# A graph network's third stage: projection from two half-state tiles, and a new order of work on four engines

## The chip, the cores and the metric

The kernel runs on one core of a Trainium2 chip. The metric is device time of one execution, in microseconds. Four engines compute: TensorE (PE) multiplies matrices, VectorE (DVE) and ScalarE (ACT) work elementwise, GpSimd (POOL) issues the gathers and scatters. SyncE (SP) issues the other transfers, which 16 DMA engines carry out. Each engine takes its own instructions in order and waits on semaphores for the others.

## The reference

Four graph layers follow each other over 100,000 nodes with 64 features and 50,000 edges. Before each layer the node state is normed: h = relu(layernorm(x)). The change lies in the third stage of the kernel, which ends the second layer and prepares the third:

```python
# second layer, its end: out is the sum over a node's edges
out = (out - mean) * rsqrt(var + eps) * gamma + beta
x = x + gelu(out + h)                       # exact gelu
# third layer, its start
h = relu(layernorm(x))
qkv = h @ qkv_w + qkv_b
qe = q[src] * 8 ** -0.5 + edge_attr @ q_rpe_w + q_rpe_b
ke = k[dst] + edge_attr @ k_rpe_w + k_rpe_b
ve = v[dst] + edge_attr @ v_rpe_w + v_rpe_b
compat = sum over 8 of qe * ke              # 4 heads
```

## The kernel before

The program runs stage by stage; between stages all engines meet. The stage in question is `conv_edges` (scope `l2`, L1588 to L1783). The edges are sorted by destination and cut into 98 **chunks** of CE = 512. A chunk's state is held turned: 64 features of the source node in partitions 0 to 63, 64 of the destination in 64 to 127, 512 edges as columns.

For a chunk, in this order: SyncE loads the edges' own rows, `keep`, and the turned states `h1` and `x1`; GpSimd gathers the rows of the destination's last edge. TensorE transposes the rows into `p_oT` (L1782). VectorE runs a scan backwards over the destination half (L1708), so that all edges of a node get its sum, and forms z = p_oT * scale + h1 (L1720). ScalarE applies gelu (L1679). VectorE adds x1: x2 (L1704). TensorE centers x2 with one matmul over 512 columns (L726), ScalarE squares (L730), TensorE averages the squares (L734, the variance), ScalarE makes 1/sqrt of it with Ln and Exp (L741, L743), VectorE scales and clips to `hT` (L748). TensorE also transposes x2 back (L1771), VectorE copies it to rows (L1728) and SyncE stores it. The 18 edge attributes with a column of ones are transposed to 32 x 512 (L1021) and copied to `ea.T` by VectorE (L1732). The **projection** takes, for each of four tiles of 128 edges, two matmuls into the same 128 columns: hT (128 rows) with `w_qkv` (L1747), and 19 rows of ea.T with `w_rpe`, added to it (L1748). ScalarE copies the result out: queries and keys `qk` (L1672), values `vc` (L1673). VectorE multiplies queries and keys (L1714) and sums over 8 (L1723); SyncE stores `vc`.

Gelu is in another table set of ScalarE than Ln and Exp, so a set is loaded (L205) before the gelu and one after it.

The order is written out by hand. The helper `slots` lets every engine run through slots; in slot s a body gets the chunks s, s-1, s-2 and so on (k0, k1, k2 ...), None where there is none. Before the change SyncE loads chunk s; TensorE works on s-2 (center, variance, back), s-4 (projection in two halves, the variance between them) and s (transposes); ScalarE on s-3 (Ln, Exp), s-5 (copies out), s-2 (square), s-1 (gelu); VectorE on s-2 (x2), s-1 (scan, z), s-5 (product, sum), s-3 (row copy, attributes, scaling). Two slots are a turn. `p_oT`, `p_back`, `p_ea`, `n_p_var` and, before, `z` are single buffers; most others are double (`u`), the loaded ones fourfold (`q`). `hold` is a wait with an empty instruction behind it.

## Time and profile before

| | us |
|---|---|
| median of the runs | 6815.0 |
| lowest and highest of 3 | 6811.4, 6820.2 |
| the profiled execution, its own time | 6795.7 |
| its span in the profile | 6793.8 |
| the stage's scans, first to last | 2861.4 to 3544.5 |

The profile is of one execution. Its time is 19 us under the median; 2 us of it lie outside the span. Busy shares over the whole span are TensorE 62%, VectorE 69%, ScalarE 49%, GpSimd 66%, but they are averages over stages with different limits, so the stage has to be read by itself.

### The profile page before, as it was taken

To read this page: it belongs to the slowest core of one execution; us is meant where nothing else is said; L and a number is where in the kernel's file an instruction comes from. 1 tells how busy PE (TensorE), PEld (TensorE's weight loads), DVE (VectorE), ACT (ScalarE), POOL (GpSimd) and SP (SyncE) were. 2 spreads that over 40 slices of the span, in tenths; PEclk is the share of its full clock that TensorE was granted. 3 is DMA by queue.
4 is the path that set the end of the run, shared out by engine and by line. 5 is a ranking of instruction groups with operands and counts; after the bars stand their busy time and mean duration, and the time that the engine had idled before them with its cause. 6 is when DMAs were issued, how large, how long until landed. Compare 5 with 4: busy or idle time off the path is not lost. (4 is left out here: it accounts for less than half of the span.)

```text
span 6793.8 us, 85831 instructions
## 1 busy us (share of the span) xinstructions
PE 4193.3 (62%) x15111; PEld 2135.7 (31%) x15111; DVE 4701.1 (69%) x9073; ACT 3325.8 (49%) x5670; POOL 4502.1 (66%) x4877
## 2 busy tenths in 40 slices
PE   0102555555477777699996777775777677777700
PEld 0000211111133333266663333332434344444400
DVE  5885888888577777576664555555777667766667
ACT  1112444444355555487885666665777733333300
POOL 4777888888644444265546888886766477777744
PEclk9999999999999999799997888887999978778855
DMA  2442222222344444499983344443333233333377
GB/s 89 140 144 56 81 74 74 78 74 74 83 132 131 132 132 129 104 186 193 192 178 93 114 114 114 114 114 93 75 80 78 65 66 71 69 71 69 69 297 309
DMA packets 949964, 773.07 MB, mean 114 GB/s; under 512 B 661199, under 2 KB 727708, under 8 KB 945875
## 3 DMA queue, kind: packets, MB, share of 16 engines
q1 hardware_dynamic: 819859, 614.72, 30.6%
q0 software_dynamic: 125504, 131.83, 12.2%
q10 hardware_dynamic: 4512, 25.60, 0.9%
q14 instruction: 66, 0.54, 0.0%
q8 instruction: 23, 0.38, 0.0%
HBM read 472.43 MB, written 310.28 MB: 115 GB/s over the span
## 5 line engine op out<-in xcount | busy, mean ns | idle before, releaser
L205 ACT ACT_TABLE_LOAD x621 | 796.7, 1283 | 139.3 <-PEq L66 128.6
L954 POOL DMA_INDIRECT x<-l_out,l_snum x392 | 472.5, 1205 | 106.5 <-issue 90.1
L918 POOL DMA_INDIRECT l_rows<-x,l_num x392 | 441.2, 1126 | 153.5 <-issue 93.7
L954 POOL DMA_INDIRECT m<-l2s_out,l2s_snum x392 | 439.2, 1120 | 146.5 <-issue 105.7
L1159 POOL DMA_INDIRECT pre_src_rows<-in_x,all_idx_src x392 | 397.2, 1013 | 164.3 <-issue 130.0
L918 POOL DMA_INDIRECT l_rows<-in_x,l_num x392 | 432.1, 1102 | 105.7 <-issue 90.6
L918 POOL DMA_INDIRECT l3a_rows<-m,l3a_num x392 | 398.6, 1017 | 144.3 <-issue 93.3
L918 POOL DMA_INDIRECT l2s_rows<-vc_rows,l2s_num x392 | 416.5, 1062 | 106.3 <-issue 95.5
L918 POOL DMA_INDIRECT l_rows<-eo,l_num x392 | 387.5, 989 | 147.7 <-issue 96.7
L954 POOL DMA_INDIRECT xg<-l3b_out,l3b_snum x392 | 395.2, 1008 | 113.2 <-issue 90.3
L918 POOL DMA_INDIRECT l3b_rows<-g_rows,l3b_num x392 | 385.6, 984 | 106.2 <-issue 92.4
L837 DVE TENSOR_TENSOR_SCAN l2s_sums<-l2s_ex,l2s_sums 128x512 f32<-128x512 f32 x97 | 124.6, 1284 | 458.3 <-ACT l2s_ex L828 458.3
L1349 PE MATMUL l_p_hT<-all_ident,l_h 128*128 128x128 f32 x392 | 109.2, 433 | 468.5 <-DVE l_h L681 468.5
L2407 PE MATMUL l3b_p_gate<-all_w_gate,l3b_acc 128*128 128x256 f32 x784 | 305.4, 557 | 32.5 <-DVEq L2366 31.4
L310 ACT ACTIVATE prep_pay<-prep_pay 128x512 f32<-128x512 f32 x136 | 85.7, 630 | 416.9 <-DVEq L396 416.9
L734 PE MATMUL l_n_p_var<-l_n_sq,all_w_mean 128*128 128x512 f32 x392 | 220.7, 645 | 95.9 <-ACT l_n_sq L730 95.6
L2399 PE MATMUL l3b_p<-all_ident,l3b_hm 128*128 128x128 f32 x392 | 126.6, 345 | 231.0 <-DVEq L2359 231.0
L1349 PEld LDWEIGHTS l_p_hT<-all_ident,l_h 128*128 128x128 f32 x392 | 70.0, 217 | 631.6 <-DVE l_h L681 631.6
L432 PE MATMUL prep_ptk<-all_ident,prep_key 128*128 128x128 f32 x72 | 20.1, 434 | 402.2 <-DVEq L382 402.2
L1981 PE MATMUL l2s_p_score<-l2s_vT,all_w_head 68*128 68x512 f32 x196 | 110.3, 645 | 238.9 <-ACT l2s_vT L1918 238.9
L1708 DVE TENSOR_TENSOR_SCAN l_p_oT<-l_keep,l_end_T,l_p_oT 64x512 f32<-64x512 f32 x98 | 127.5, 1301 | 185.5 <-PE l_p_oT L1782 148.2
L2454 POOL TENSOR_TENSOR dl_min<-dl_min,all_shift 128x1600 f32<-128x1600 f32 x32 | 131.2, 4099 | 182.7 <-DMA dl_min<-m 182.7
(407 smaller groups left out, 13700.1 us busy)
## 6 DMA issues: line engine op xcount, KB each, us to landing
l_far<-far_d SPq DMA_DIRECT2D x196, 256.0 KB, 3.4
xg<-l2s_bg_row SPq DMA_DIRECT2D x97, 512.0 KB, 3.8
dl_xin<-xg SPq DMA_DIRECT2D x31, 1600.0 KB
l2s_bg_x<-x SPq DMA_DIRECT2D x97, 260.0 KB, 3.0
x<-ts_row SPq DMA_DIRECT2D x31, 812.5 KB, 4.4
l_keep<-keep_d SPq DMA_DIRECT2D x196, 128.0 KB, 2.9
xs<-l_xT SPq DMA_DIRECT2D x98, 256.0 KB, 2.7
hs<-l_hT SPq DMA_DIRECT2D x98, 256.0 KB, 3.0
```

The costliest lines, as they stand in the source:

```text
L205: act.add_instruction(mybir.InstLoadActFuncSet(name=nc.get_next_instruction_name(), ins=[], outs=[], act_func_set_id=which))
L734: pe.matmul(self.p_var[:], c.w_mean[:], self.sq[:], start=True, stop=True).then_inc(self.spread, 1)
L837: dve.tensor_tensor_scan(self.sums[k.u][:], self.ex[:, 0, :], self.ex[:, 1, :], 0.0 if k.start else self.sums[1 - k.u][:, CE - 1:CE], ALU. ...
L918: pool.indirect_dma_start(self.buf[k.q][:, j, at:at + w], None, table, bass.IndirectOffsetOnAxis(ap=self.num[k.q][:, m, j:j + 1], axis=0)) ...
L954: pool.indirect_dma_start(self.table, bass.IndirectOffsetOnAxis(ap=self.num[k.q][:, j:j + 1], axis=0), self.out[k.q][:, j, 0:self.cols], N ...
L1159: pool.indirect_dma_start(c.src_rows[:, t, :], None, x, bass.IndirectOffsetOnAxis(ap=c.idx_src[:, t:t + 1], axis=0)).then_inc(c.src_gather ...
L1349: ins = pe.transpose(p_hT[:, j * P:(j + 1) * P], h[:, j, :], c.ident[:])
L1708: swept = step(dve.tensor_tensor_scan(p_oT[D:P, ::-1], keep[k1.q][D:P, ::-1], p_oT[D:P, ::-1], end_T[D:P, bass.ds(k1.i, 1)], ALU.mult, ALU ...
L1981: pe.matmul(p_score[k1.u][:], c.w_head[:], vT[k1.u][:], start=True, stop=True).then_inc(m["scored"], 1)
L2399: pe.transpose(p_01[:, cols], hm[:, j, 0:P], c.ident[:])
L2407: ins = pe.matmul(p_gates[:, j, :], acc[k1.u][:, j * P:(j + 1) * P], c.w_gate[:], start=True, stop=True)
L2454: pool.tensor_tensor(min_[k.u][:], min_[k.u][:], over_rows(c.shift3[0:NP, :], NR), ALU.add).then_inc(pool_done, 1)
```

## The change

Destination and source half of the normed state go to two tiles, each of which also holds the attributes: `from_src` has the source half in partitions 0 to 63 and the attributes in 64 to 95; `from_dst` has the attributes in 0 to 31 and the destination half in 64 to 127, with zeros between. The weights are copied together once to match (`w_q`, `w_kv`). The projection is then, for each tile, one matmul of 96 rows into 32 columns (the queries) and one of 128 rows into 96 columns (keys and values), neither added to the other. VectorE scales in two instructions (`scale_halves`); ScalarE copies the attributes, twice, in place of VectorE's one copy. z gets a second buffer. Gelu of chunk s-2 stands at the end of ScalarE's even slots and at the start of the odd ones, so that two gelus share one table load. Center, variance, square and what follows move by one slot; the variance becomes TensorE's last work in a slot, the new chunk's transposes stand ahead of it, and the projection is in one piece. ScalarE's copies out stand behind the square. SyncE loads x1 and the attributes two slots after the rows.

```diff
+    def scale_halves(self, dve, k, top, bottom):
+
+        dve.wait_ge(self.scaled, k.n)
+        cen, rstd = self.of(self.p_cen, k), self.of(self.rstd, k)
+        dve.scalar_tensor_tensor(top[0:D, :], cen[0:D, :], 0.0, rstd[0:D, :], ALU.max, ALU.mult)
+        dve.scalar_tensor_tensor(bottom[D:P, :], cen[D:P, :], 0.0, rstd[D:P, :], ALU.max, ALU.mult).then_inc(self.done, 1)
...
-        z, hT = s.sb("z", [P, CE]), [s.sb(f"hT{u}", [P, CE]) for u in range(2)]
+        z = [s.sb(f"z{u}", [P, CE]) for u in range(2)]
+        from_src, from_dst = ([s.sb(f"{n}{u}", [P, CE]) for u in range(2)] for n in ("from_src", "from_dst"))
+        w_q, w_kv = s.sb("w_q", [P, 32]), s.sb("w_kv", [P, 96])
...
-        ea = EdgeAttr(s, edge_attr, ATTR, 1, both=True)
+        ea = EdgeAttr(s, edge_attr, ATTR, 1)
...
-                def body(k, k1, _2, _3, old, _5, _6, older):
+                def body(k, _1, k2, _3, _4, old, _6, _7, older):
...
-                        if not k.round:
-                            hold(sp, m["x2_ready"], k.n - 4)
-                        sp.dma_start(x1[k.q][:], feature_rows(xs, k)).then_inc(x1_loaded[k.q], 16)
+                    if k2:
+                        if not k2.round:
+                            hold(sp, m["x2_ready"], k2.n - 4)
+                        sp.dma_start(x1[k2.q][:], feature_rows(xs, k2)).then_inc(x1_loaded[k2.q], 16)
                     if old:
                         hold(sp, m["rows_ready"], old.n)
                         sp.dma_start(edge_rows(x2e, old), x2_rows[old.u][:]).then_inc(x2_saved[old.u], 16)
...
-                    if k1:
-                        ea.load(sp, c, k1)
-                slots(sp, c.NCH, 7, body)
+                    if k2:
+                        ea.load(sp, c, k2)
+                slots(sp, c.NCH, 8, body)
...
-                def body(k1, k2, k3, k5):
+                def gelu(k):
+                    act.wait_ge(m["z_ready"], k.n)
+                    act.activation(z[k.u][:], z[k.u][:], ACT.Gelu, bias=c.shift1T[:, 0:1]).then_inc(m["gelu_done"], 1)
+
+                def attributes(k):
+                    if not k.first:
+                        act.wait_ge(m["qkv_done"], k.n - 2)
+                    act.wait_ge(ea.turned, k.n)
+                    act.activation(from_src[k.u][D:D + 32, :], ea.p[:], ACT.Copy)
+                    act.activation(from_dst[k.u][0:32, :], ea.p[:], ACT.Copy).then_inc(ea.ready, 1)
...
+                def out(k):
+                    if not k.first:
+                        act.wait_ge(m["vc_ready"], k.n - 2)
+                    if not k.round:
+                        act.wait_ge(vc_saved[k.q], 16 * k.r)
+                    act.wait_ge(m["qkv_done"], k.n)
+                    v = p_qkv[k.u][:].rearrange("p (j f) -> p j f", j=TPC)
+                    act.activation(qk[k.u][:], v[:, :, 0:D], ACT.Copy)
+                    act.activation(vc[k.q][:, :, 0:D], v[:, :, D:P], ACT.Copy).then_inc(m["qkv_out"], 1)
+
+                def even(k2, k3, k4, k6):
+                    if k4:
+                        norm.rsqrt(act, c, k4)
+                    load_set(nc, act, GELU_SET)
+                    if k4:
+                        attributes(k4)
                     if k3:
-                        norm.rsqrt(act, c, k3)
-                    if k5:
-                        if not k5.first:
-                            act.wait_ge(m["vc_ready"], k5.n - 2)
-                        if not k5.round:
-                            act.wait_ge(vc_saved[k5.q], 16 * k5.r)
-                        act.wait_ge(m["qkv_done"], k5.n)
-                        v = p_qkv[k5.u][:].rearrange("p (j f) -> p j f", j=TPC)
-                        act.activation(qk[k5.u][:], v[:, :, 0:D], ACT.Copy)
-                        act.activation(vc[k5.q][:, :, 0:D], v[:, :, D:P], ACT.Copy).then_inc(m["qkv_out"], 1)
-                    load_set(nc, act, GELU_SET)
-                    if k2:
-                        norm.square(act, k2)
-                    if k1:
-                        act.wait_ge(m["z_ready"], k1.n)
-                        act.activation(z[:], z[:], ACT.Gelu, bias=c.shift1T[:, 0:1]).then_inc(m["gelu_done"], 1)
+                        norm.square(act, k3)
+                    if k6:
+                        out(k6)
+                    if k2:
+                        gelu(k2)
+
+                def odd(k2, k3, k4, k6):
+                    if k2:
+                        gelu(k2)
                     load_ln_exp(nc, act)
-                slots(act, c.NCH, 5, lambda k0, k1, k2, k3, k4, k5: body(k1, k2, k3, k5))
+                    if k4:
+                        attributes(k4)
+                    if k3:
+                        norm.square(act, k3)
+                    if k4:
+                        norm.rsqrt(act, c, k4)
+                    if k6:
+                        out(k6)
+                calls = [0]
+
+                def body(_0, _1, k2, k3, k4, _5, k6):
+                    calls[0] += 1
+                    (even if calls[0] % 2 else odd)(k2, k3, k4, k6)
+                slots(act, c.NCH, 6, body)
...
+                for w_ in (w_q, w_kv):
+                    early(dve.memset(w_[:], 0.0))
+                early(dve.tensor_copy(w_q[0:D, :], c.w_qkv[0:D, 0:32]))
+                early(dve.tensor_copy(w_q[D:D + ATTR + 1, :], c.w_rpe[0:ATTR + 1, 0:32]))
+                early(dve.tensor_copy(w_kv[0:ATTR + 1, :], c.w_rpe[0:ATTR + 1, 32:P]))
+                early(dve.tensor_copy(w_kv[D:P, :], c.w_qkv[D:P, 32:P]))
+                for u in range(2):
+                    early(dve.memset(from_dst[u][:], 0.0))
...
+                def body(k1, k3, k4, k6):
+                    if k3:
+                        if not k3.first:
+                            dve.wait_ge(m["back_turned"], k3.n - 2)
+                        dve.wait_ge(x1_loaded[k3.q], 16 * (k3.r + 1))
+                        dve.wait_ge(m["gelu_done"], k3.n)
+                        dve.tensor_tensor(x2[k3.u][:], z[k3.u][:], x1[k3.q][:], ALU.add).then_inc(m["x2_ready"], 1)
                     if k1:
                         dve.wait_ge(keep_loaded[k1.q], 16 * (k1.r + 1))
                         dve.wait_ge(rows.rows_free, k1.n)
                         swept = step(dve.tensor_tensor_scan(p_oT[D:P, ::-1], keep[k1.q][D:P, ::-1], p_oT[D:P, ::-1],
                                                             end_T[D:P, bass.ds(k1.i, 1)], ALU.mult, ALU.add))
...
+                    if k6:
+                        if not k6.start:
+                            dve.wait_ge(m["vc_ready"], k6.n - 1)
+                        dve.wait_ge(m["qkv_out"], k6.n)
+                        multiplied = step(dve.tensor_tensor(prod[:].rearrange("p j h f -> p j (h f)"), qk[k6.u][:, :, 0:32],
+                                                            qk[k6.u][:, :, 32:64], ALU.mult))
                     if k1:
                         step.ended(swept)
                         dve.sem_inc(m["keep_used"], 1)
+                        if not k1.first:
+                            dve.wait_ge(m["x2_ready"], k1.n - 2)
                         dve.wait_ge(h1_loaded[k1.q], 16 * (k1.r + 1))
-                        dve.scalar_tensor_tensor(z[:], p_oT[:], c.scale1T[:, 0:1], h1[k1.q][:], ALU.mult, ALU.add).then_inc(m["z_ready"], 1)
-                    if k5:
+                        dve.scalar_tensor_tensor(z[k1.u][:], p_oT[:], c.scale1T[:, 0:1], h1[k1.q][:], ALU.mult, ALU.add).then_inc(m["z_ready"], 1)
+                    if k6:
                         step.ended(multiplied)
...
+                        dve.tensor_reduce(vc[k6.q][:, :, D:VC], prod[:], AX, ALU.add).then_inc(m["vc_ready"], 1)
+                    if k4:
+                        if not k4.first:
+                            dve.wait_ge(x2_saved[k4.u], 16 * k4.t)
+                        dve.wait_ge(m["back_turned"], k4.n)
+                        dve.tensor_copy(x2_rows[k4.u][:].rearrange("p j f -> p (j f)"), p_back[:]).then_inc(m["rows_ready"], 1)
+                        if not k4.first:
+                            dve.wait_ge(m["qkv_done"], k4.n - 2)
+                        norm.scale_halves(dve, k4, from_src[k4.u], from_dst[k4.u])
+                slots(dve, c.NCH, 6, lambda k0, k1, k2, k3, k4, k5, k6: body(k1, k3, k4, k6), step)
...
-                hold(pe, m["early_step"], 8)
+                hold(pe, m["early_step"], 16)
...
                 def project(k, tiles):
                     for j in tiles:
                         at = slice(j * P, (j + 1) * P)
-                        pe.matmul(p_qkv[k.u][:, at], hT[k.u][:, at], c.w_qkv[:], start=True, stop=False)
-                        ins = pe.matmul(p_qkv[k.u][:, at], ea.T[k.u][0:ATTR + 1, at], c.w_rpe[:], start=False, stop=True)
+                        pe.matmul(p_qkv[k.u][:, j * P:j * P + 32], from_src[k.u][0:D + 32, at], w_q[0:D + 32, :], start=True, stop=True)
+                        ins = pe.matmul(p_qkv[k.u][:, j * P + 32:(j + 1) * P], from_dst[k.u][:, at], w_kv[:], start=True, stop=True)
                     return ins
...
-                def body(k0, k1, k2, k3, k4):
-                    if k2:
-                        hold(pe, m["x2_ready"], k2.n)
-                        norm.center(pe, c, k2, x2[k2.u][:])
-                    if k4:
-                        if not k4.first:
-                            hold(pe, m["qkv_out"], k4.n - 2)
-                        hold(pe, ea.ready, k4.n)
-                        hold(pe, norm.done, k4.n)
-                        project(k4, (0, 1))
-                    if k2:
-                        if k3:
-                            hold(pe, norm.logged, k3.n)
-                        norm.variance(pe, c, k2)
-                    if k4:
-                        project(k4, (2, 3)).then_inc(m["qkv_done"], 1)
-                    if k2:
-                        if k3:
-                            hold(pe, m["rows_ready"], k3.n)
+                def body(k0, k1, _2, k3, k4, k5):
+                    if k3:
+                        hold(pe, m["x2_ready"], k3.n)
+                        norm.center(pe, c, k3, x2[k3.u][:])
+                    if k5:
+                        if not k5.first:
+                            hold(pe, m["qkv_out"], k5.n - 2)
+                        hold(pe, ea.ready, k5.n)
+                        hold(pe, norm.done, k5.n)
+                        project(k5, range(TPC)).then_inc(m["qkv_done"], 1)
+                    if k3:
+                        if k4:
+                            hold(pe, m["rows_ready"], k4.n)
                         for j in range(TPC):
-                            ins = pe.transpose(p_back[:, j * P:(j + 1) * P], x2[k2.u][:, j * P:(j + 1) * P], c.ident[:])
+                            ins = pe.transpose(p_back[:, j * P:(j + 1) * P], x2[k3.u][:, j * P:(j + 1) * P], c.ident[:])
                         ins.then_inc(m["back_turned"], 1)
-                        if k3:
-                            hold(pe, ea.ready, k3.n)
-                        ea.turn(pe, c, k2)
                     if k0:
                         if k1:
                             hold(pe, m["z_ready"], k1.n)
@@ -1781,7 +1822,14 @@
                         for j in range(TPC):
                             ins = pe.transpose(p_oT[:, j * P:(j + 1) * P], rows.buf[k0.q][:, j, :], c.ident[:])
                         ins.then_inc(rows.rows_free, 1)
-                slots(pe, c.NCH, 4, body)
+                    if k3:
+                        if k4:
+                            hold(pe, ea.ready, k4.n)
+                        ea.turn(pe, c, k3)
+                        if k4:
+                            hold(pe, norm.logged, k4.n)
+                        norm.variance(pe, c, k3)
+                slots(pe, c.NCH, 5, body)
```

On ScalarE, the steady part of the stage, before: one slot. Names end in the buffer's number; `l2_n_sq` is the square, `l2_n_rstd` Ln and Exp, `l2_z` gelu, `l2_qk` and `l2_vc` the copies out.

```order
L741 ACTIVATE l2_n_rstd0<-l2_n_p_var,all_eps 128x512
L743 ACTIVATE l2_n_rstd0<-l2_n_rstd0 128x512
L1672 ACTIVATE l2_qk0<-l2_p_qkv0 128x256
L1673 ACTIVATE l2_vc0<-l2_p_qkv0 128x4x64
L205 ACT_TABLE_LOAD
L730 ACTIVATE l2_n_sq<-l2_n_p_cen1 128x512
L1679 ACTIVATE l2_z<-l2_z,all_shift1T 128x512
L205 ACT_TABLE_LOAD
```

After, from the copies out of an even slot to those of the odd one behind it (`from_src`, `from_dst` are the attribute copies):

```order
L1690 ACTIVATE l2_qk0<-l2_p_qkv0 128x256
L1691 ACTIVATE l2_vc2<-l2_p_qkv0 128x4x64
L1674 ACTIVATE l2_z0<-l2_z0,all_shift1T 128x512
L1674 ACTIVATE l2_z1<-l2_z1,all_shift1T 128x512
L205 ACT_TABLE_LOAD
L1680 ACTIVATE l2_from_src1<-l2_p_ea 32x512
L1681 ACTIVATE l2_from_dst1<-l2_p_ea 32x512
L730 ACTIVATE l2_n_sq<-l2_n_p_cen0 128x512
L741 ACTIVATE l2_n_rstd1<-l2_n_p_var,all_eps 128x512
L743 ACTIVATE l2_n_rstd1<-l2_n_rstd1 128x512
L1690 ACTIVATE l2_qk1<-l2_p_qkv1 128x256
L1691 ACTIVATE l2_vc3<-l2_p_qkv1 128x4x64
```

The copies out stand behind the square now; in the odd slot behind Ln and Exp too, and one table load stands between two gelus and the next Ln.

On TensorE, the same part, one slot before (`l2_p_oT` are the transposes of the new chunk, `l2_p_back` those of x2):

```order
L1747 MATMUL l2_p_qkv1<-all_w_qkv,l2_hT1 128x128
L1748 MATMUL l2_p_qkv1<-all_w_rpe,l2_eaT1 128x128
L1747 MATMUL l2_p_qkv1<-all_w_qkv,l2_hT1 128x128
L1748 MATMUL l2_p_qkv1<-all_w_rpe,l2_eaT1 128x128
L734 MATMUL l2_n_p_var<-l2_n_sq,all_w_mean 128x512
L1747 MATMUL l2_p_qkv1<-all_w_qkv,l2_hT1 128x128
L1748 MATMUL l2_p_qkv1<-all_w_rpe,l2_eaT1 128x128
L1747 MATMUL l2_p_qkv1<-all_w_qkv,l2_hT1 128x128
L1748 MATMUL l2_p_qkv1<-all_w_rpe,l2_eaT1 128x128
L1771 MATMUL l2_p_back<-all_ident,l2_x2_1 128x128 x4
L1021 MATMUL l2_p_ea<-all_ident,l2_ea1 32x128 x4
L1782 MATMUL l2_p_oT<-all_ident,l2_rows1 128x128 x4
```

And after, the end of one slot, with the last tile's projection, from which the next slot follows with the center (the first row is a keys-and-values matmul of the slot):

```order
L1798 MATMUL l2_p_qkv1<-l2_w_kv,l2_from_dst1 128x96
L1797 MATMUL l2_p_qkv1<-l2_w_q,l2_from_src1 128x32
L1798 MATMUL l2_p_qkv1<-l2_w_kv,l2_from_dst1 128x96
L1815 MATMUL l2_p_back<-all_ident,l2_x2_1 128x128 x4
L199 REGISTER_ALU
L1823 MATMUL l2_p_oT<-all_ident,l2_rows2 128x128 x4
L1028 MATMUL l2_p_ea<-all_ident,l2_ea1 32x128 x4
L734 MATMUL l2_n_p_var<-l2_n_sq,all_w_mean 128x512
```

The variance has moved from the projection's middle to the slot's end, behind the back-transposes, the new chunk's transposes and the attributes.

## Rows read from the trace of the kernel before

**Rows 1.** Instructions of the tile p_oT: min/median/max ns, first and last start in us.

```profile
L1708 DVE TENSOR_TENSOR_SCAN l_p_oT<-l_keep,l_end_T,l_p_oT x98: 1300/1301/1302, 2861.4 to 3544.5; 64x512 f32<-64x512 f32 x98
```

**Rows 2.** Timeline 3205 to 3216: start us, us, engine, line, operation, count [idle before <-releaser].

```profile
3207.53 0.69 ACT L741 ACTIVATE l_n_rstd<-l_n_p_var,all_eps 128x512 f32<-128x512 f32 x1 [0.22 <-PE l_n_p_var L734]
...
3208.25 0.63 ACT L743 ACTIVATE l_n_rstd<-l_n_rstd 128x512 f32<-128x512 f32 x1
...
3208.83 0.66 PE L1771 MATMUL l_p_back<-all_ident,l_x 128*128 128x128 f32 x4
3209.02 0.38 ACT L1672 ACTIVATE l_qk<-l_p_qkv 128x256 f32<-128x256 f32 x1
...
3209.30 0.38 ACT L1673 ACTIVATE l_vc<-l_p_qkv 128x256 f32<-128x256 f32 x1
3209.33 0.60 PE L1021 MATMUL l_p_ea<-all_ident,l_ea 128*32 128x128 f32 x4
...
3209.70 1.28 ACT L205 ACT_TABLE_LOAD   x1
3209.76 0.60 PE L1782 MATMUL l_p_oT<-all_ident,l_rows 128*128 128x128 f32 x4
...
3210.20 1.02 PE L726 MATMUL l_n_p_cen<-l_x,all_w_center 128*128 128x512 f32 x2
...
3210.51 1.30 DVE L1708 TENSOR_TENSOR_SCAN l_p_oT<-l_keep,l_end_T,l_p_oT 64x512 f32<-64x512 f32 x1 [2.69 <-PE l_p_oT L1782]
...
3211.06 0.38 PE L1747 MATMUL l_p_qkv<-all_w_qkv,l_hT 128*128 128x128 f32 x2
...
3211.26 0.60 ACT L730 ACTIVATE l_n_sq<-l_n_p_cen 128x512 f32<-128x512 f32 x1 [0.28 <-PE l_n_p_cen L726]
...
3211.79 0.49 PE L1747 MATMUL l_p_qkv<-all_w_qkv,l_hT 128*128 128x128 f32 x2
3211.84 0.29 DVE L1714 TENSOR_TENSOR l_prod<-l_qk 128x128 f32<-128x128 f32 x1
3212.17 0.75 DVE L1720 SCALAR_TENSOR_TENSOR l_z<-l_p_oT,all_scale1T,l_h 128x512 f32<-128x512 f32 x1
...
3212.83 0.28 DVE L1723 TENSOR_REDUCE l_vc<-l_prod 128x16 f32<-128x128 f32 x1
3212.95 0.72 ACT L1679 ACTIVATE l_z<-l_z,all_shift1T 128x512 f32<-128x512 f32 x1 [1.09 <-DVE l_z L1720]
...
3213.03 0.68 DVE L1728 COPY l_x_rows<-l_p_back 128x512 f32<-128x512 f32 x1
...
3215.14 0.66 PE L1771 MATMUL l_p_back<-all_ident,l_x 128*128 128x128 f32 x4
```

**Rows 3.** Stretches: us, busy of PE, PEld, DVE, ACT, POOL (count), granted clock, DMA share, GB/s.

```profile
3240.00:3340.00 100.00, 93.19 (x459) 62.18 (x458) 70.19 (x114) 83.54 (x118) 59.59 (x72) 0.98 0.99 193
...
5000.00:5300.00 300.00, 228.96 (x902) 120.46 (x902) 226.41 (x587) 237.91 (x407) 193.01 (x227) 1.00 0.35 79
5800.00:6100.00 300.00, 228.14 (x821) 130.43 (x822) 209.01 (x437) 94.85 (x176) 238.66 (x284) 0.80 0.34 70
```

**Rows 4.** Waits between 3000 and 3500: us in total, times, longest.

```profile
DVE l_p_oT L1708 <- PE l_p_oT L1782: 112.9, 62, 6.7
```

**Rows 5.** DMA queue of SyncE, 3000 to 3500: packets, MB, share of 16 engines.

```profile
q1 hardware_dynamic: 174856, 86.28, 66.0%
```

**Rows 6.** The attributes' copy in the stage before, by its line.

```profile
L1026 ACT ACTIVATE l_eaT<-l_n_p_var x98: 587/587/587, 1820.6 to 2807.8; 32x512 f32<-32x512 f32 x98
```

**Rows 7.** Groups by line, 3000 to 3500: count, busy us, mean ns, idle before.

```profile
L1771 PE MATMUL l_p_back<-all_ident,l_x 128*128 128x128 f32 x284 | 47.4, 290 | 2.4 <-DVE l_x_rows L1728 2.4
```

**Rows 8.** The page's costliest groups, transposes of the first and of the last edge stage.

```profile
L1349 PE MATMUL l_p_hT<-all_ident,l_h 128*128 128x128 f32 x392 | 109.2, 433 | 468.5 <-DVE l_h L681 468.5
...
L2399 PE MATMUL l3b_p<-all_ident,l3b_hm 128*128 128x128 f32 x392 | 126.6, 345 | 231.0 <-DVEq L2359 231.0
```

24 lines of the change are left out of this document (removed).

## The prediction

> **What bounds the kernel now.** I first placed the stage. The view of one tile's instructions shows the scan of the gathered rows once for each of the 98 chunks, from 2861.4 to 3544.5 us [rows 1]: 97 steps of 7.04 us, 683 us of 6794. The change touches nothing else, so everything below is about the length of one such step, a slot. Then I read one undisturbed slot in order of time [rows 2]: TensorE's transposes of x2 start at 3208.83 and again at 3215.14, so the pace without a disturbance is 6.31 us. In it TensorE has hardly a gap. The busy table agrees: TensorE 93 us of 100, ScalarE 84, VectorE 70 [rows 3]. The waits do too: the largest one of the stage is VectorE's scan waiting for TensorE's transposes, 112.9 us in 500 [rows 4]. So today TensorE sets the pace. The 0.73 us by which the mean slot is longer come from elsewhere: the hardware queue's packets take 66.0% of 16 DMA engines' time [rows 5], the engines' busy share is 0.99 [rows 3], and now and then a load lands late.
>
> The order of work is written out by hand and every engine takes its queue strictly in order. So two prices must be read: each engine's own work in a slot, and the longest closed chain of waits across engines, divided by the slots that it spans. Before, no closed chain is as long as TensorE's own work.
>
 Which of them holds decides nothing here, since the projection turns out to lie beside the longest chain.
> [...]
>
> **ScalarE.** Out goes one of two table loads a slot, 1.28 us; in come two copies of the attributes, 32x512 each, 0.59 us each by the same form in the stage before [rows 6]. Own sum after, from starts in [rows 2]: load 1.28, Ln 0.72, Exp 0.65, two copies 1.17, square 0.60, the two output copies 0.28 + 0.38, gelu 0.72: 5.8 us. Before it was 5.9. Nothing gained by itself.
>
> **VectorE.** One copy of 32x512 goes, and the scaling of the normed state becomes two instructions on 64 partitions. At worst both cost what the whole did. VectorE's busy time is then that of before, 70% of 7.04 = 4.9 us. Bounds: a copy less to a few tenths more; both beside the chain below.
>
> **The moved order, and the chain that it closes.** Call a slot s. After the change VectorE's slot s holds, in this order: x2 of chunk s-3, scan of s-1, product of s-6, z of s-1, sum of s-6, copy of the turned-back rows of s-4, the two scalings. The product of s-6 waits for ScalarE's output copies of s-6, which now stand in ScalarE's slot s **behind** the square of s-3. z stands behind the product. TensorE's slot s is: center s-3, projection s-5, back-transposes s-3 (they wait for VectorE's row copy of s-4), transposes of the new chunk s, attributes, and **last** the variance of s-3. ScalarE's even slots begin with the Ln of s-4, which waits for that variance, made in TensorE's slot s-1. So from the end of ScalarE's output copies to the end of the next ones everything hangs on one chain. With the starts of [rows 2]:
> - output copies done, product starts: 0.10 (z to gelu shows 0.03, transposes to scan 0.15); product to z 0.33; z to sum 0.66; sum to row copy 0.20; row copy 0.68; to TensorE 0.15. Together 2.12 us.
> - back-transposes 0.50, the two other groups of four 0.43 + 0.44: 1.37 us. Then the variance. Same shape as the center, which holds the engine 0.86 us and whose square starts 1.06 us after it.
> - Even slot: Ln starts at 2.12 + 1.37 + 1.06 = 4.55; then Ln 0.72, Exp 0.65, table load 1.28, two copies 1.17, square 0.60, output copies 0.28 + 0.38: 5.08. Sum **9.6 us**.
> - Odd slot: gelu, load and attribute copies are done in the shadow (they end near 4.4). The center of the next chunk stands behind the variance, at 2.12 + 1.37 + 0.86 = 4.35; its square starts at 5.41; square 0.60, Ln 0.72, Exp 0.65, output copies 0.66. Sum **8.0 us**.
>
> Mean 8.8 us a slot with TensorE at full clock, against 7.04 now. What hid these steps before: the output copies stood ahead of the square, the center of a chunk ran while ScalarE loaded tables, the variance was made between the projection's halves with a slot to spare before its Ln. x2 is not late: z to x2's end is about 3 us of VectorE's work, so x2 is there 3.8 us after the copies, before TensorE asks at 4.35.
>
> **TensorE's clock.** The projection ends 4.35 + 0.86 + 1.8 = 7.0 us after the output copies; the next back-transposes start at 8.0 + 2.1 = 10.1 in an odd slot and 9.6 + 2.1 = 11.7 in an even one. So TensorE sits idle for 3 to 5 us in each slot. In the last edge stage it idles 231.0 us before 392 transposes, its granted clock is 0.80 there against 0.98 in our stage and 1.00 in the stage that idles little [rows 3], and the same kind of transpose takes 290 ns in the mean in our stage [rows 7] and 345 there; in the first stage, with 468.5 us of idle, 433 ns [rows 8]. [...] On the chain TensorE has 1.37 + 0.86 us in each slot and 0.86 more in every other: 2.7 us. Bounds: nothing at half clock, 8.8; all of it, 8.8 + 2.7 = 11.5. The nearest row is the last edge stage (gaps of similar length): half of it, 8.8 + 1.35 = **10.2 us**.
> [...]
>
> **The rest.** SyncE's loads move to the chunks' new lags: x1 and attributes are issued two slots after the rows, and each is still a slot ahead of its use. At 10.2 us a slot the DMA engines have more time than today, so the 0.73 us of late loads goes; it is in the 7.04 that I subtract from. GpSimd's gathers wait for the transposes as before (its own work is under 60 us in 100 [rows 3]). The start has eight more small VectorE steps, ahead of a wait for a gather on which VectorE stands anyway: nothing, or 2 us if that cover is gone. One more slot of lag at the end, with little in it: 7 us (bounds 3 and 10).
>
> **Sum**, against the profiled execution, 6795.7 us: 97 x (10.2 - 7.04) = 306, and 7 for the lag: 7109. The median of the runs shown, 6815.0, is 19 us above that execution, so I forecast 7128.
>
> **Rivals.**
> 1. The chain holds but the clock stays up: 8.8 us, 97 x 1.79 + 7 = 181, so 6996; less 2% of the chain, if my start-to-start times carry a little slack, 6978. For it: the stage with 76% busy TensorE at 1.00. Against it: gaps of 3 to 5 us. Chance 0.22.
> 2. All of the chain at half clock: 11.5 us, 7255. For it the 433 ns of the first stage, whose gaps are as long. Against it: at that pace TensorE is again busy 80% of the time. Chance 0.12.
> 3. The other side: the chain does not close, because the output copies find their projection a slot earlier and VectorE never stands at the product; then the longest own sum rules, ScalarE's 5.8 us and some waiting, 6.0 us: 97 x (6.0 - 7.04) + 7 = -94, so 6721. It decides at the point where the chain is under 7.04 us a slot, 1.8 us less than the rows give. Only one of ten terms would have to be gone, but each is an instruction that stands in order. Chance 0.03. The row for it is that ScalarE's slot of before (5.9) and VectorE's (4.9) are well under TensorE's.
> 4. The slot happens to end within 0.14 us of 7.04, no change: 0.01.
> 5. That the change does not do what it says: the printed order shows one table load a slot and the new operands, so I give it nothing.
>
> **How the numbers follow.** My own case, slots of 9.3 to 11.2 us, 7045 to 7225, has 0.62. The range of 8 in 10 takes rival 1 with the low bound of its sum and rival 2: 6970 to 7255. Faster by over 0.2% 0.03, within 0.2% 0.01, slower 0.96; 0.2%, 14 us, is about what a measurement of this kernel can tell from no change.
>
> **What would show it.** In the changed profile: scans 9 to 11 us apart, alternately longer and shorter by some 1.6 us; ScalarE waiting before the Ln for the variance in even slots, before the square for the center in odd ones; VectorE waiting longest before the product, for ScalarE's copy; TensorE waiting before the back-transposes for the row copy; its granted clock near 0.8; DMA share clearly below 0.9. About half as many table loads in the stage. I am wrong if the slots are about 6 us with ScalarE nearly full, and wrong on the clock alone if they are 8.8.

## The result and the profile after

The changed kernel takes 7106.8 us, the kernel before 6813.2: ratio 1.0427, 95% interval 1.0406 to 1.0447, so 4.3% slower. Forecast: 7128, range 6970 to 7255. The profiled execution took 7108.7 us, 313.0 more than that of before. One of the four runs of the changed kernel took 7974.5 us, in a slower state of the chip, and the ratio leaves it out.

Scans and sums of the stage, as [rows 1], [rows 3], [rows 4] and [rows 5] (the windows in the last two stages are taken 240 and 300 us later, since what follows our stage begins some 309 us later); first the tile's scan with first and last start, then stretches, then waits from 3000 to 3500, then SyncE's queue:

```profile
L1758 DVE TENSOR_TENSOR_SCAN l_p_oT<-l_keep,l_end_T,l_p_oT x98: 1300/1301/1303, 2862.6 to 3835.5; 64x512 f32<-64x512 f32 x98
```

```profile
3240.00:3340.00 100.00, 69.05 (x316) 48.80 (x314) 48.05 (x75) 54.60 (x90) 40.80 (x50) 0.74 0.59 131
...
5240.00:5540.00 300.00, 228.87 (x902) 120.30 (x900) 226.84 (x589) 237.87 (x409) 192.75 (x226) 1.00 0.35 79
6100.00:6400.00 300.00, 221.68 (x812) 126.18 (x812) 207.22 (x436) 94.04 (x174) 238.47 (x284) 0.82 0.34 70
```

```profile
DVE l_prod L1764 <- ACT l_vc L1691: 241.5, 49, 6.0
...
PE l_p_back L1815 <- DVE l_x_rows L1780: 162.3, 49, 4.5
ACT l_n_rstd L741 <- PE l_n_p_var L734: 132.5, 24, 6.7
```

```profile
q1 hardware_dynamic: 120385, 59.73, 46.4%
```

97 steps take 972.9 us, 10.03 each: 289.8 us more than before. No engine is busy more than 69% of the stretch, the granted clock fell from 0.98 to 0.74, the DMA share from 0.99 to 0.59; the rows of the other two stages are nearly their old ones. ScalarE loads a table set 101 times in the stage, 205 times before. The three waits are those of the forecast chain, each with all its slots (24 Ln, one in every other slot). Another 18 us lie behind the last scan (48 from it to VectorE's first instruction of the next stage, 30 before), 1 ahead of the first, and 4 are spread.

Now two slots in order of time. This one has TensorE at full clock (granted 1.00 from 3380.6 to 3390.1) and ends with the even kind of ScalarE's turn:

```profile
3380.60 0.29 DVE L1764 TENSOR_TENSOR l_prod<-l_qk 128x128 f32<-128x128 f32 x1 [4.65 <-ACT l_vc L1691]
...
3381.79 0.68 DVE L1780 COPY l_x_rows<-l_p_back 128x512 f32<-128x512 f32 x1
...
3382.62 0.63 PE L1815 MATMUL l_p_back<-all_ident,l_x 128*128 128x128 f32 x4 [2.71 <-DVE l_x_rows L1780]
...
3383.96 1.02 PE L734 MATMUL l_n_p_var<-l_n_sq,all_w_mean 128*128 128x512 f32 x2
...
3384.82 1.02 PE L726 MATMUL l_n_p_cen<-l_x,all_w_center 128*128 128x512 f32 x2
3385.09 0.69 ACT L741 ACTIVATE l_n_rstd<-l_n_p_var,all_eps 128x512 f32<-128x512 f32 x1 [4.51 <-PE l_n_p_var L734]
...
3388.84 0.57 ACT L730 ACTIVATE l_n_sq<-l_n_p_cen 128x512 f32<-128x512 f32 x1
...
3390.05 0.29 DVE L1764 TENSOR_TENSOR l_prod<-l_qk 128x128 f32<-128x128 f32 x1 [4.22 <-ACT l_vc L1691]
```

And this one is odd and at half clock (granted 0.50 from 3310.1 to 3312.5, and again 0.50 from 3312.72 to 3314.63):

```profile
3308.13 0.29 DVE L1764 TENSOR_TENSOR l_prod<-l_qk 128x128 f32<-128x128 f32 x1 [4.22 <-ACT l_vc L1691]
...
3310.14 1.08 PE L1815 MATMUL l_p_back<-all_ident,l_x 128*128 128x128 f32 x4 [4.45 <-DVE l_x_rows L1780]
...
3312.72 1.91 PE L734 MATMUL l_n_p_var<-l_n_sq,all_w_mean 128*128 128x512 f32 x2
...
3314.43 1.79 PE L726 MATMUL l_n_p_cen<-l_x,all_w_center 128*128 128x512 f32 x2
...
3316.26 0.60 ACT L730 ACTIVATE l_n_sq<-l_n_p_cen 128x512 f32<-128x512 f32 x1 [2.04 <-PE l_n_p_cen L726]
...
3318.74 0.29 DVE L1764 TENSOR_TENSOR l_prod<-l_qk 128x128 f32<-128x128 f32 x1 [5.22 <-ACT l_vc L1691]
```

The reader is to see the same chain twice: product, row copy, back-transposes, variance, and from there Ln (even) or center and square (odd), then the output copies and the next product. The even slot takes 9.45 us, forecast 9.6 for full clock; the odd one 10.61, forecast 8.0 for full clock. Its steps on TensorE take 2.85 us more than in that sum: from the product to the center 6.30 us, 4.22 in the first slot, and from the center to the square 1.83, forecast 1.06. ScalarE's steps behind the square take 0.25 less than in the sum (2.48, forecast 2.73 to the next product).

### The profile page after: what moved, and what is told of

Its sections match the earlier page's. It is cut to its first block and busy times, and to the rows that moved or that the text cites. A ratio compares the mean times of both kernels' runs of the same rounds, so it can differ in the third digit from the quotient of the medians.

```text
span 7106.7 us, 86254 instructions
## 1 busy us (share of the span) xinstructions
PE 4210.1 (59%) x15111; PEld 2180.7 (31%) x15111; DVE 4720.5 (66%) x9081; ACT 3289.3 (46%) x5762; POOL 4496.0 (63%) x4877
## 5 line engine op out<-in xcount | busy, mean ns | idle before, releaser
L925 POOL DMA_INDIRECT l_rows<-eo,l_num x392 | 372.7, 951 | 142.2 <-issue 95.9
L1764 DVE TENSOR_TENSOR l_prod<-l_qk 128x128 f32<-128x128 f32 x98 | 28.7, 293 | 477.0 <-ACT l_vc L1691 476.9
L734 PE MATMUL l_n_p_var<-l_n_sq,all_w_mean 128*128 128x512 f32 x392 | 283.2, 814 | 90.6 <-ACT l_n_sq L730 90.6
L741 ACT ACTIVATE l_n_rstd<-l_n_p_var,all_eps 128x512 f32<-128x512 f32 x196 | 134.5, 686 | 350.7 <-PE l_n_p_var L734 350.7
L913 POOL COPY l_num<-all_idx_pos 128x4 int32 (+1 forms) x98 | 28.4, 290 | 405.4 <-PE l_p_oT L1823 405.4
L1815 PE MATMUL l_p_back<-all_ident,l_x 128*128 128x128 f32 x392 | 89.9, 373 | 312.4 <-DVE l_x_rows L1780 312.4
```

The costliest lines, as they stand in the source:

```text
L734: pe.matmul(self.p_var[:], c.w_mean[:], self.sq[:], start=True, stop=True).then_inc(self.spread, 1)
L741: act.activation(rstd[:], self.p_var[:], ACT.Ln, bias=c.eps[:, 0:1]).then_inc(self.logged, 1)
L925: pool.indirect_dma_start(self.buf[k.q][:, j, at:at + w], None, table, bass.IndirectOffsetOnAxis(ap=self.num[k.q][:, m, j:j + 1], axis=0)) ...
L1815: ins = pe.transpose(p_back[:, j * P:(j + 1) * P], x2[k3.u][:, j * P:(j + 1) * P], c.ident[:])
```

## The experiments

Where nothing else is said, they start from the changed kernel. Ratios are to the kernel before on the same chip, with 95% intervals.

**Output copies ahead of the square.**

```diff
 def even(k2, k3, k4, k6):
+    if k6: out(k6)
     if k4: norm.rsqrt(act, c, k4)
...
-    if k6: out(k6)
     if k2: gelu(k2)
 def odd(k2, k3, k4, k6):
     if k2: gelu(k2)
+    if k6: out(k6)
     load_ln_exp(nc, act)
...
-    if k6: out(k6)
```

> The changed kernel with one edit: ScalarE's two output copies of the chunk of six slots ago stand ahead of its attribute copies and its square (first in the even slots, behind gelu in the odd ones). Nothing is added or taken away. Theory A, the closed chain: the product of VectorE no longer waits for the square, so the chain from output copies over VectorE, the transposes and the variance back to the output copies is open; what is left is ScalarE's own 5.9 us a slot and the loads, so slots of 6.3 to 7.0 us, granted clock in the stage above 0.9, and 7107 - 97 x (10.03 - 6.65) = 6779 us, between 6745 and 6825. Theory B, the new work itself is the cost (attribute copies on ScalarE, scaling in halves, gelus in pairs): all of it is still there, slots stay at 10.0 us and the time at 7107 within 30. Theory C, the clock alone is the cause: TensorE has no more to do than before, so its clock stays at 0.8 and the time within 7050 to 7107.

Measured: 6818.3 us, ratio 1.0018 (1.0008 to 1.0027), some 280 us less than the changed kernel. Its trace from 3000 to 3500:

```profile
3000.00:3500.00 500.00, 408.12 (x2221) 289.50 (x2220) 358.08 (x555) 375.08 (x626) 288.03 (x348) 0.90 0.98 188
```

The DMA share is back at 0.98 and the slots at 7.15 us. One move of two instructions takes nearly all of the loss away, with every new instruction still there. Theories B and C fall. The middle of the expectation was 40 us too low. The pace is close to that of before the change (7.04), no engine is busy more than 82% of the stretch, and the DMA share is 0.98, so I take the loads to set it; that slots get shorter with cheaper stores, further down, bears it out.

**Variance behind the projection**, ahead of the wait for the row copy.

```diff
                         project(k5, range(TPC)).then_inc(m["qkv_done"], 1)
                     if k3:
+                        if k4: hold(pe, norm.logged, k4.n)
+                        norm.variance(pe, c, k3)
                         if k4: hold(pe, m["rows_ready"], k4.n)
...
                         ea.turn(pe, c, k3)
-                        if k4: hold(pe, norm.logged, k4.n)
-                        norm.variance(pe, c, k3)
```

> The changed kernel with the variance directly behind the projection on TensorE, ahead of the back-transposes; all else as changed. Theory A: the Ln of the even slots no longer hangs on the row copy and the transposes (4.5 us of the even slot's 9.6), and in the odd slots the center comes 0.86 us earlier; the rest of the chain stays. Longest chain 7.1 us a slot at full clock and 7.3 at the clock of this kernel: 7107 - 97 x (10.03 - 7.3) = 6842, between 6810 and 6890; a wait for the row copy is still seen on TensorE. Theory B: 7107 within 30. Theory C: no more TensorE work, so no gain beyond 60 us.

Measured: 6840.4, ratio 1.0041 (1.0028 to 1.0054). As worked out. TensorE still waits 82.9 us of 500 for the row copy, against 162.3.

**Row copy ahead of the scan.**

```diff
+                    if k4: # back_turned k4, then
+                        dve.tensor_copy(x2_rows[k4.u][:].rearrange("p j f -> p (j f)"), p_back[:]).then_inc(m["rows_ready"], 1)
                     if k1: # scan, then product of k6, z of k1, sum of k6
...
-                        dve.tensor_copy(x2_rows[k4.u][:].rearrange("p j f -> p (j f)"), p_back[:]).then_inc(m["rows_ready"], 1)
```

> The changed kernel with another single edit: VectorE's copy of the turned-back rows stands ahead of the scan instead of behind product, z and sum. Theory A: TensorE's back-transposes then don't wait for the product, so the same chain is cut at another place; ScalarE's own work and the loads are left, slots of 6.3 to 7.1 us, 6745 to 6830 us, about 6790. A chain in which the output copies were the only culprit (behind the square) would still show VectorE waiting at the product, but not TensorE at the back-transposes. Theory B: 7107 within 30. Theory C: 7050 to 7107 with the clock at 0.8.

Measured: 6952.3, ratio 1.0208 (1.0186 to 1.0230): half of what I expected. The waits from 3000 to 3500 say why:

```profile
DVE l_prod L1769 <- ACT l_vc L1691: 187.5, 58, 4.7
...
PE l_p_oT L1824 <- DVE l_z L1777: 140.5, 58, 3.5
ACT l_n_rstd L741 <- PE l_n_p_var L734: 111.5, 29, 5.3
```

TensorE no longer waits for the row copy but for z. Its transposes of the new chunk go into the single buffer `p_oT`, which z reads, and z stands behind the product. I had overlooked that second tie. So the product was put behind z too (`multiplied = step(...)` with its waits moves behind the instruction that makes z):

> The run with the row copy ahead of the scan gained only half of what was expected, and its trace shows TensorE waiting for z (140 us of 500) instead of for the row copy: the transposes of the new chunk go into the single buffer that z reads, and z still stands behind the product. So here the product goes behind z too: VectorE's order is x2, row copy, scan, z, product, sum, scalings. Theory A: now nothing that TensorE waits for stands behind the product, the longest chain is 6.4 us a slot at full clock and 7.0 at a clock of 0.8; with the loads as in the run with the early output copies (7.15 us a slot) the slots are 6.9 to 7.3 us and the time 6790 to 6845, about 6820. If the reason of the shortfall was another one (the clock, the variance's place), the time stays near 6950 within 30 us.

Measured: 6813.4, ratio 1.0015 (1.0004 to 1.0026). The chain is open at this place as well.

**More work on TensorE.**

```diff
+                        for _ in range(2):
+                            project(k5, range(TPC))
                         project(k5, range(TPC)).then_inc(m["qkv_done"], 1)
```

> The changed kernel with the projection made three times over instead of once (same operands, same place, same values), 16 more matmul instructions a slot, 3.5 us of TensorE work in what was idle time ahead of the back-transposes. Order and waits are as changed. Theory A with the clock as its second part: idle stretches of 2.7 to 4.5 us shrink to 0 to 1.2, the granted clock of the stage goes from 0.75 to above 0.95, back-transposes take 0.43 us for four in every slot, and the slots come down from 10.2 to the chain at full clock, 8.9 to 9.2 (the odd slots may overrun by 0.5): 7107 - 97 x 1.05 = 7005, between 6985 and 7035. So more work would be faster. If the clock plays no part (theory B, or a chain whose TensorE terms don't matter): 7107 to 7140. Theory C, the clock is the whole cause: back to 6815.

Measured: 7011.4, ratio 1.0296 (1.0275 to 1.0317), some 90 us faster with 3.5 us more TensorE work in each slot. Scans, stretch, back-transposes, and one product with the back-transposes behind it:

```profile
L1758 DVE TENSOR_TENSOR_SCAN l_p_oT<-l_keep,l_end_T,l_p_oT x98: 1300/1302/1302, 2861.6 to 3735.1; 64x512 f32<-64x512 f32 x98
```

```profile
3000.00:3500.00 500.00, 477.77 (x3494) 410.96 (x3493) 280.96 (x439) 295.36 (x487) 221.82 (x273) 0.97 0.67 148
```

```profile
L1817 PE MATMUL l_p_back<-all_ident,l_x 128*128 128x128 f32 x220 | 36.4, 292 | 22.0 <-DVE l_x_rows L1780 22.0
```

```profile
3200.90 0.29 DVE L1764 TENSOR_TENSOR l_prod<-l_qk 128x128 f32<-128x128 f32 x1 [4.21 <-ACT l_vc L1691]
...
3203.55 0.60 PE L1817 MATMUL l_p_back<-all_ident,l_x 128*128 128x128 f32 x4
```

The clock is 0.97 (0.75 in the changed kernel from 3000 to 3500), a transpose takes 292 ns (373 in the changed kernel), the slots are mostly 7.9 and 10.0 us by turns, where the forecast for full clock was 8.0 and 9.6. From the eleventh slot on they are 9.1 us in the mean, in the changed kernel 10.2: of the 3.2 us by which a slot is longer than before, the clock makes at least 1.1 and the order of work the rest. At least, because the repeated projection costs something itself: in the longer slots it ends late, and the back-transposes start 2.65 us after the product, 2.02 in the changed kernel's full-clock slot. That is 0.6 us in every other slot, 0.3 a slot; without it the clock would be worth about 1.4.

**The order alone, in the kernel before.** Tiles, projection, table loads and lags stay.

```diff
 ScalarE:
                     if k3: norm.rsqrt(act, c, k3)
-                    if k5: # waits, qk and vc
                     load_set(nc, act, GELU_SET)
                     if k2: norm.square(act, k2)
+                    if k5: # waits, qk and vc
 TensorE:
-                        project(k4, (0, 1))
-                    if k2: # norm.logged k3, then norm.variance(pe, c, k2)
-                    if k4: project(k4, (2, 3)).then_inc(m["qkv_done"], 1)
+                        project(k4, range(TPC)).then_inc(m["qkv_done"], 1)
...
                         ins.then_inc(rows.rows_free, 1)
+                    if k2: # norm.logged k3, then norm.variance(pe, c, k2)
```

> The kernel before, its tiles, its projection, its two table loads and its lags untouched, with only two moves of the change: ScalarE's output copies stand behind the square, and TensorE's variance is its last work in a slot (the projection in one piece). Theory A: these two together close the same kind of chain. By the durations of the rows each alone would give about 7.0 us a slot, both together 8.7 at full clock and 9.2 at a clock of 0.8. TensorE keeps its own 6.3 us a slot, so it idles less than in the changed kernel: 6807 + 97 x (8.7 to 9.4 - 7.04) = 6970 to 7040, about 7000. Theory B, the new tiles, halves and attribute copies are the cost: none of them is here, so 6807 within 30.

Measured: 7096.8, ratio 1.0445 (1.0429 to 1.0462). As slow as the whole change, and some 60 us beyond my upper end. One slot:

```profile
3205.93 0.63 PE L1765 MATMUL l_p_back<-all_ident,l_x 128*128 128x128 f32 x4 [1.90 <-DVE l_x_rows L1728]
...
3206.71 1.01 PE L1021 MATMUL l_p_ea<-all_ident,l_ea 128*32 128x128 f32 x4 [0.15 <-issue]
...
3207.52 1.06 PE L1776 MATMUL l_p_oT<-all_ident,l_rows 128*128 128x128 f32 x4
3208.37 1.88 PE L734 MATMUL l_n_p_var<-l_n_sq,all_w_mean 128*128 128x512 f32 x2
```

After only 1.9 us of idle time the clock halves from the second group on (granted 1.00 from 3205.93 to 3206.56, 0.52 from 3206.7 to 3210.2), and so it does in each slot of the stretch from 3000 to 3500: the four back-transposes' records are 281 ns in the mean, those of the variance 1034 (656 in the kernel before), and the granted clock is 0.83. That is 0.4 + 0.4 + 0.9 us on top of 8.7, which makes 10.4; the slots are 10.1 to 10.4. The size of the clock term was wrong, the chain was not.

**The tiles and the projection alone, in the order of before**, both attribute copies on VectorE:

```diff
-                        dve.tensor_copy(ea.T[k3.u][:], ea.p[:]).then_inc(ea.ready, 1)
-                        norm.scale_to(dve, k3, hT[k3.u][:])
+                        dve.tensor_copy(from_src[k3.u][D:D + 32, :], ea.p[:])
+                        dve.tensor_copy(from_dst[k3.u][0:32, :], ea.p[:]).then_inc(ea.ready, 1)
+                        norm.scale_halves(dve, k3, from_src[k3.u], from_dst[k3.u])
```

> The other part alone: the kernel before in its own order, with the two tiles of half states, the 96- and 128-row operands and the scaling in halves. VectorE makes both attribute copies (it made one), ScalarE none. TensorE's projection falls from 2.9 to 1.8 us a slot, to 5.2 us in all; VectorE's own work rises from 4.9 to 6.2. Theory A: no chain is closed, so nothing is lost, and with TensorE out of the way the loads and VectorE are the floor: slots of 6.6 to 7.1 us, 6765 to 6815, about 6795. Theory B, the new work is what costs the 300 us: 6950 or more.

Measured: 6790.0, ratio 0.9989 (0.9980 to 0.9998), 7.6 us faster. The stretch from 3000 to 3500:

```profile
3000.00:3500.00 500.00, 401.34 (x2255) 283.07 (x2255) 460.56 (x710) 406.44 (x565) 292.02 (x355) 0.95 1.00 192
```

TensorE is busy 80% instead of 93% [rows 3], and the time hardly moves: the DMA share is 1.00, and VectorE, with the added copy and the halves, is busy 92%. Which of the two holds the slot at 7.02 us this run does not say, and so it stays open whether TensorE alone held the kernel before, as the prediction reads it. Three of the change's costs (two attribute copies, though here on VectorE, halves, a projection of another form) are all here, and nothing is lost.

**A version that beats both.** With the loads as the floor, first both moves together:

> Both edits together: output copies ahead of the square and of the attribute copies, and the variance behind the projection. Each alone gave 6818 and 6840 us. Theory A with the loads as the floor: the chain is 5.8 us a slot, well under the loads, so nothing more than the output copies alone gave, 6795 to 6825 us, DMA share 0.98. If what is left in the run with early output copies were still a chain of waits (0.2 us less a slot by the sum), 6760 to 6790.

Measured: 6839.0, ratio 1.0047 (1.0031 to 1.0062), 21 us slower than the output copies alone, against both expectations. The cause stays open: VectorE waits more there for late loads of x1 (79.4 us of 500 against 58.5). Then longer stored pieces, 2048 bytes of x2 instead of 512 and 1088 of the values instead of 272 (the store of `vc`, the other operand and the back-transposes change in the same way):

```diff
+def edge_quads(table, k):
+    return table[bass.ds(k.i * CE, CE), :].rearrange("(p j) f -> p j f", j=TPC)
...
-sp.dma_start(edge_rows(x2e, old), x2_rows[old.u][:])
+sp.dma_start(edge_quads(x2e, old), x2_rows[old.u][:])
...
-from_src[k.u][0:D + 32, at]
+from_src[k.u][0:D + 32, :].rearrange("f (p j) -> f j p", j=TPC)[:, j, :]
```

> The same two edits, and the two stores of the stage made of longer pieces: a partition's four rows of a chunk lie next to each other in memory (edges 4p to 4p+3 instead of p, p+128, ...), so x2's rows leave in 128 packets of 2048 bytes instead of 512 of 512, the values in 128 of 1088 instead of 512 of 272. The back-transposes and the projection take every fourth column for it. By the trace a packet of 512 bytes takes 27 ns, one of 272 bytes 19, one of 2048 bytes 84, so some 6.8 us of packet time over 16 engines, 0.43 us a slot. If the loads and stores are the floor of the stage (DMA share 0.98 in it): 97 x 0.43 = 41 us less than the same kernel without it, 6740 to 6785, about 6768. If the floor is a chain of waits or an engine: no difference, 6795 to 6825. If the columns taken in steps of four cost TensorE time: more.

Measured: 6783.5, ratio 0.9969 (0.9959 to 0.9979). The same stores in the kernel before:

> The kernel before with only the longer pieces in its two stores. Its TensorE work is 6.31 us a slot and its slots 7.04. If the 0.73 us between them are late loads, as the prediction says, 0.43 us of packet time a slot less gives 20 to 41 us: 6766 to 6787 us. If they are something else: 6807 within 7. If columns in steps of four are dearer for TensorE, more than 6807, since TensorE is nearly full there.

Measured: 6897.9, ratio 1.0138 (1.0121 to 1.0155). Stretch and weight loads of the projection in it, the same loads in the kernel before (3000 to 3500), then the stretch of the run with longer pieces in the changed kernel:

```profile
3000.00:3500.00 500.00, 500.00 (x1970) 392.83 (x1968) 304.69 (x496) 361.41 (x494) 255.10 (x310) 1.00 0.67 167
```

```profile
L1757 PEld LDWEIGHTS l_p_qkv<-all_w_qkv,l_hT 128*128 128x128 f32 x496 | 143.6, 313 | 59.7 <-issue 29.6
```

```profile
L1747 PEld LDWEIGHTS l_p_qkv<-all_w_qkv,l_hT 128*128 128x128 f32 x566 | 99.2, 195 | 90.1 <-issue 73.5
```

```profile
3000.00:3500.00 500.00, 500.00 (x2345) 429.44 (x2344) 376.59 (x585) 398.80 (x659) 298.74 (x360) 0.97 0.80 199
```

The DMA share falls to 0.67 and 0.80, so the stores are indeed cheaper; but TensorE is busy without a gap, since a weight load over every fourth column takes 313 ns (195 in the kernel before). That is the third case of the expectation, the dear columns. So VectorE was made to write the state in the stored order, and the projection reads whole columns again:

```diff
-top[0:D, :], cen[0:D, :], 0.0, rstd[0:D, :]
+tiles(top[0:D, :]), quads(cen[0:D, :]), 0.0, quads(rstd[0:D, :])
```

Here `tiles` views a row of 512 as 4 x 128 in place, `quads` takes every fourth column first. The attributes are loaded in the same order.

> The kernel with the longer stored pieces took 22 us less than the kernel before, and its trace shows the DMA share down from 0.98 to 0.80 and TensorE busy in 500 us of 500: a weight load over every fourth column takes 0.32 us in the mean against 0.21. Here the projection reads whole columns again: VectorE's scaling writes the normed state in the order of the stored pieces (it reads every fourth column), and the attributes are loaded in that order, so only the four back-transposes of a slot still load in steps of four. Theory: the 8 strided loads of the projection were the bound; TensorE's own work falls from 6.8 to about 5.3 us, the loads stay below 0.9 of the time, ScalarE's 5.9 us a slot is next, slots of 6.0 to 6.5 us: 6784 - 97 x (6.80 - 6.25) = 6731, 6705 to 6765. If the strided reads are as dear for VectorE (three scalings' worth of time more), slots stay at 6.8 and the time at 6784 within 15.

Measured: 6735.9, ratio 0.9912 (0.9898 to 0.9927). And without the moved variance:

> The same without the moved variance (it is TensorE's last work in a slot, as changed; only the output copies are moved). In the kernels bound by loads the moved variance cost 20 us, though the sum of the chain is 0.1 us shorter with it. If that was an effect of late loads, which are gone here, this kernel is equal to the one with the moved variance or up to 30 us slower (chain 5.9 against 5.8 us at full clock, 6.3 against 6.0 at 0.8): 6715 to 6790, about 6745. If the moved variance costs by itself, this one is the faster of the two by 20.

Measured: 6736.7, ratio 0.9915 (0.9901 to 0.9928). The moved variance costs nothing by itself here. The stretch of the run with the moved variance, one of its scalings (every fourth column read) and a weight load of its projection:

```profile
3000.00:3500.00 500.00, 412.21 (x2526) 311.37 (x2524) 466.80 (x630) 428.75 (x709) 293.62 (x363) 0.98 0.91 210
```

```profile
L756 DVE SCALAR_TENSOR_TENSOR l_from_src<-l_n_p_cen,l_n_rstd 64x512 f32<-64x512 f32 x79 | 85.9, 1087 | 9.7 <-ACT l_n_rstd L743 9.6
...
L1815 PEld LDWEIGHTS l_p_qkv<-l_w_kv,l_from_dst 128*128 128x128 f32 x636 | 98.9, 195 | 0.0
```

Both are 0.9% faster than the kernel before and some 5% faster than the changed one; VectorE is now the fullest engine, 467 of 500 us.

## Why the prediction was right, and where not

- **The stage and the mechanism.** The loss is in this stage, 290 of 313 us, and comes from the closed chain: opening it by one move gives some 280 us back, and closing it in the kernel before costs 299 without any other part of the change. TensorE's, VectorE's and ScalarE's waits stand where the prediction put them.
- **The chain's length.** 8.8 us at full clock was forecast. The run with the repeated projection has 9.1, with a few half-clock slots in it and 0.3 of its own delay, and the full-clock slot above reproduces the terms one by one: product to row copy 1.19, to back-transposes 0.83, to the variance 1.34, to Ln 1.13, to the next product 4.96.
- **The clock.** I took half of TensorE's 2.7 us on the chain at half clock, 1.35 a slot. Steady slots are 10.2, so it was 1.1 against the 9.1 of the run with more work, 1.4 against the sum or with that run's own delay taken off. That half of it would run at half clock was my estimate from one other stage at 0.80, and no run shows such a share there; what the runs showed in its place is these 1.1 to 1.4 us a slot. The estimate came out well: in the kernel before with its closed chain the clock cost 1.5 us, though TensorE idles less there. The ground given for it is weaker than it reads: the stage at clock 1.00 is said to idle little, but by [rows 3] TensorE was busy 228.96 of 300 us there and 228.14 in the stage at 0.80, so the share of busy time does not tell the two apart.
- **By turns longer and shorter by 1.6 us**: wrong. Counted from product to product in a steady stretch of eight, the odd slots are 9.8 to 10.6 and the even ones 9.4 to 11.4, in the mean 10.1 and 10.4. The half clock falls mostly on the odd slots, all four of which begin at it behind 3.5 to 4.5 us of idle time; of the even ones, behind 2.7 to 2.8, one does. That evens them out.
- **The projection** takes 8 x 2 passes of 0.11 us, 1.76 us: the lower bound of the two. It decided nothing, as forecast. In the trace each of its eight matmuls is two records, as before (784 of L1797 and of L1798 for 392 matmuls each). A tile starts 0.44 us after the one before it, against 0.73 to 0.83 before; operands, widths and the adding up all changed at once, and no run shows which of them gave how much.
- **The end** cost 18 us, not 7 (bounds 3 and 10): the last slots hang on the same chain instead of running empty. **Slots** cost 290, not 306, since the first six are still 4.3 to 8.3 us long. The two errors cancel to some 5 us, and the 5 us ahead of the first scan and spread take up the rest: that the sum gave 313 us for the profiled execution and 313.0 were measured is luck. The 21 us between 7128 and 7106.8 are mostly the 19 added for the median of before; the changed kernel's profiled execution is no faster than its median.
- **The rivals.** The clock staying up (6996) is what the repeated projection shows, 7011. All at half clock came in one slot of eight (11.44 us). The open chain came only by moving work, and with the output copies or with row copy and product moved it stopped at 7.1 us a slot with the DMA share at 0.98 and 0.99, not at ScalarE's 6.0, so rival 3's 6721 would have been too low too.

## What to carry to other kernels

Where each engine takes its queue in order, sum the longest closed chain of waits across engines, not only each engine's work: two small moves (copies behind a square, a matmul to the end) cost 300 us together in the kernel before, and taking back either of them in the changed one gave 260 to 280 back. Before a shorter projection or a saved table load is worth anything, look at what else is at 0.98 in that stage. And on a chain that leaves TensorE idle, price its terms at both levels of the clock (here the variance's two records took 1.02 us at a granted 1.00 and 1.91 at 0.50).

## What the hardware showed that I had not expected

- TensorE fell to half clock (granted 0.52 from 3206.7 to 3210.2) behind idle stretches of only 1.9 us, once in each slot, in a stretch in which it was busy 80% of the time (the closed chain in the kernel before); and repeating matmuls for nothing made the changed kernel 1.3% faster.
- fp32 operands read in steps of four elements were slow: a weight load of the projection took 313 ns, against 195 in the kernel before, a VectorE instruction over 64 x 512 1087 ns, against 673 in the changed kernel. What makes them slow no run shows; the VectorE instruction reads two operands in such steps, one from SBUF and one from PSUM, and no run takes them apart.
- Packets of 2048 bytes in place of 512 and 1088 in place of 272 took the stage's DMA share from 0.96 to 0.80 at a shorter slot, though they carry the same bytes. The smaller part of that is the stores' own: from 3000 to 3500 SyncE's queue took 63.6% of the DMA engines' time for 67 stored chunks and then 64.2% for 73, while the gathers' queue fell from 32.6% (267 gathers) to 15.5% (289). The same gathers took half the time, so a DMA share near 1 is not all work that has to be done.
